# ODE stage of a mixed convolution and attention kernel: chunks 2 and 3 of the first product summed and split together

## The reference

```python
def _mlp(y, W1, b1, W2, b2, W3, b3):
    h = jnp.tanh(y @ W1.T + b1)          # 128 -> 512
    h = jnp.tanh(h @ W2.T + b2)          # 512 -> 512
    return h @ W3.T + b3                 # 512 -> 128

def _rk4_step(y, dt, params):
    k1 = f(y); k2 = f(y + dt / 2 * k1); k3 = f(y + dt / 2 * k2); k4 = f(y + dt * k3)
    return y + dt * (k1 + 2 * k2 + 2 * k3 + k4) / 6
# y0 = the layer-normed token 0 of each batch entry; 511 such steps, one after the other,
# give the 512 states that are added to the stream
```

## Time and profile before

| | |
|---|---|
| median of 3 runs | 10121.75 us (10118.84 to 10124.09) |
| the profiled execution | 10122.17 us |
| its span, first to last instruction | 10120.3 us |
| PE busy | 6818.0 us (67%) |
| DVE busy | 6894.7 us (68%) |
| ACT busy | 3280.2 us (32%) |
| POOL busy | 2146.6 us (21%) |
| mean granted TensorE clock, share of full speed | 0.623 |

### The profile page before, as it was taken

How to read it: one execution, slowest core, us unless ns; L and a number is a source line. 1 busy time by engine, 2 the same in 40 slices (tenths; PEclk the granted TensorE clock), 3 DMA queues, 4 the chain that set the end, 5 groups by cost and what they waited for, 6 DMA issues and landing times. The chain is left out here.

```text
span 10120.3 us, 368042 instructions
## 1 busy us (share of the span) xinstructions
PE 6818.0 (67%) x137720; PEld 5044.2 (50%) x137720; DVE 6894.7 (68%) x34057; ACT 3280.2 (32%) x11208; POOL 2146.6 (21%) x5931
## 2 busy tenths in 40 slices
PE   7886566666666666666666666666666558888888
PEld 3332455555555555555555555555555433333333
DVE  4554566666666666666666666666666479888898
ACT  3442222222222222222222222222222345555555
POOL 0000111111111111111111111111111025555554
PEclk8887555555555555555555555555555679999998
DMA  0000000000000000000000000000000000000000
GB/s 6 1 1 1 9 3 3 3 4 3 3 4 3 3 3 4 3 3 3 4 3 3 3 4 3 3 3 4 3 3 20 0 16 16 16 16 16 16 16 4
DMA packets 20732, 60.86 MB, mean 6 GB/s; under 512 B 4260, under 2 KB 13159, under 8 KB 16759
## 3 DMA queue, kind: packets, MB, share of 16 engines
q1 hardware_dynamic: 18502, 36.44, 1.0%
q0 software_dynamic: 432, 0.56, 0.0%
HBM read 35.94 MB, written 1.05 MB: 4 GB/s over the span
## 5 line engine op out<-in xcount | busy, mean ns | idle before, releaser
L565 PE MATMUL p<-H,W 128*128 128x8 f16 x130816 | 4162.8, 168 | 2547.1 <-DVE H L706 2536.6
L565 PEld LDWEIGHTS p<-H,W 128*128 128x128 f16 x130816 | 3816.6, 104 | 2893.3 <-DVE H L706 2882.4
L706 DVE SCALAR_TENSOR_TENSOR H<-h,H 128x8 f16<-128x8 f32 x10220 | 1499.7, 163 | 281.3
L641 ACT ACTIVATE h<-u 128x8 f32<-128x8 f32 x4088 | 852.1, 208 | 2490.3 <-DVE u L726 2297.5
L636 ACT ACTIVATE h<-r 128x8 f32<-128x8 f32 x4088 | 851.2, 208 | 2477.8 <-DVE r L734 2253.5
L726 DVE TENSOR_REDUCE u<-p 128x8 f32<-128x24 f32 x6132 | 1000.8, 174 | 826.4 <-PE p L565 826.4
L734 DVE TENSOR_REDUCE r<-p 128x8 f32<-128x24 f32 x4088 | 746.2, 183 | 1129.3 <-PE p L565 848.4
L701 DVE TENSOR_SCALAR H<-h 128x8 f16<-128x8 f32 x8176 | 1399.1, 171 | 38.4 <-ACT h L636 38.3
L1060 POOL TENSOR_TENSOR F<-F,dist 128x512 f32<-128x512 f32 x512 | 757.7, 1482 | 892.7 <-DVE F L1203 892.7
L541 POOL TENSOR_TENSOR twice<-r 128x16 f32<-128x16 f32 x511 | 109.8, 215 | 2932.5 <-DVE r L734 2932.5
L1197 DVE TENSOR_SCALAR qn<-dist 128x512 f32<-128x512 f32 x544 | 675.7, 1242 | 0.0
(11 more groups left out here) (290 smaller groups left out, 5598.1 us busy)
## 6 DMA issues: line engine op xcount, KB each, us to landing
W_even<-in_spline SPq DMA_DIRECT2D x12, 1024.0 KB, 6.9
W_odd<-in_spline SPq DMA_DIRECT2D x12, 1024.0 KB, 6.8
s<-in_scaler SPq DMA_DIRECT2D x24, 128.0 KB, 7.3
W_even<-in_base SPq DMA_DIRECT2D x12, 128.0 KB, 6.7
W_odd<-in_base SPq DMA_DIRECT2D x12, 128.0 KB, 6.6
xb<-in_x SPq DMA_DIRECT2D x4, 256.0 KB, 2.7
w2f<-in_ff_w SPq DMA_DIRECT2D x1, 1024.0 KB
out_x<-stream SPq DMA_DIRECT2D x1, 1024.0 KB, 4.2
```

Of the source, the lines that this page charges most:

```text
L565: ins = pe.matmul(out[:, m, 0:2 * B], W[:, q, k, P * m:P * m + P], H[:, k, :, :].rearrange("p q b -> p (q b)"), start=fresh[m], stop=(left ...
L641: sg.up(act.activation(cols(h2[:, e, :], q), cols(u2, q), ACT.Tanh, scale=scale), "h2")
L706: sg.up(dve.scalar_tensor_tensor(out=Hq[:, :, 1, :], in0=mb(cols(h, q)), scalar=HSCALE, in1=Hq[:, :, 0, :], op0=ALU.mult, op1=ALU.subtract ...
```

## The change

Chunks 2 and 3 are summed by one `tensor_reduce` after the first product and their low halves are written by one operation. PE raises `l2_ps` twice instead of three times in an evaluation, DVE `u2` and `in2` likewise, and ACT's second tanh waits for the second sum. The order of the blocks stays.

```diff
-    RED2, LOW2 = [(0, 1), (2,), (3,)], [(0, 1), (2,), (3,)]
+    RED2 = LOW2 = [(0, 1), (2, 3)]
...
-                                wait(act, "u2", len(RED2) * e + (1, 3)[n], w, i)
+                                wait(act, "u2", len(RED2) * e + n + 1, w, i)
...
-                        low(h2[:, e, :], H2, 2, (2,), at2 + 2, w, i)
-                        low(h2[:, e, :], H2, 2, (3,), at2 + 2, w, i)
+                        low(h2[:, e, :], H2, 2, (2, 3), at2 + 2, w, i)
```

## The result

The changed kernel takes **10148.96 us** (median of 10 runs, 10139.44 to 10159.43) against 10124.01 us for the kernel before in the same comparison (10 runs): ratio 1.0025, 95% interval 1.0016 to 1.0035. It is slower by 25 us, just clear of the noise, where 10114 us was forecast and the range ended at 10142. The profiled execution took 10142.68 us, 20.5 us more than the one before.

The account below looks back on a forecast made before the run. The ODE stage was taken as bound by a chain of small dependent steps through chunks 0 and 1. Merged sum 0, merged low half 0, code pauses -8 us from 10121.75 gave 10114 us, range 10088 to 10142.

Parts of the forecast that it names:

- The loop: PE-DVE-ACT chain through chunks 0 and 1: stays 1.62 us per product; merged sum and low half count 0 us.
- my own sign of being wrong: In the ODE stage: the first product's period differing from the second's would show the forecast wrong on the loop.
- The waits: DVE and PE signals: one wait fewer per evaluation each; ACT's second wait only gets a new number; counted 0 us.
- The code pauses: DVE's instruction supply: 80 instructions a step become 60, so pauses cost less, 8 us gained; bounds 32 gained, 16 lost.
- the queue: Rival: DVE's queue is on the loop, so removed operations gain 470 us, giving 9652 us; chance 2%.
- the longer sum: Rival: the merged sum, 13 ns longer, delays the high half behind it, 27 us slower, 10149 us; chance 5%.
- within 0.2%: Whole kernel: the time stays within 0.2% (about 20 us) of the kernel before; chance 77%.

Follow-up runs that it names:

- e1_early: The changed kernel with ACT's wait for POOL's sums (hsum) moved from the first tanh of line 641 to the second tanh of line 636; 10117.34 us.
- e5b_splits: The changed kernel with three separate sums again, only the low halves merged, and the second tanh's wait as before; 10128.38 us.
- e3_each: The changed kernel with the wait for hsum in all four evaluations of a step instead of one; 10235.03 us.
- e2_swap: The changed kernel with ACT's two waits in the other order, u2 first and hsum second; 10154.76 us.
- e4_sums: The changed kernel with only the sums merged, the low halves of chunks 2 and 3 staying two operations; 10161.35 us.
- e6b_pad2: e1_early plus two one-column memsets on DVE ahead of its loop, carried out once in the launch; 10105.45 us.
- e7b_pad4: e4_sums with the early wait of e1_early and four one-column memsets on DVE ahead of the loop; 10093.2 us.
- e8b_pad1: e4_sums with the early wait of e1_early and one one-column memset on DVE ahead of the loop; 10175.46 us.

## Why the prediction was wrong

**The loop: right, but for that one tanh.** PE starts 1.62 us apart in both products in three evaluations of four, the merged operations take 182 and 167 ns, and the freed DVE time is idle time (392 us less busy, where over 400 were forecast). In a step's first evaluation the first product takes 1.68 us (3737.89 to 3739.57 above), and a difference between the two periods was my own sign of being wrong. e1_early shows that both merged operations together cost the loop nothing; e5b_splits agrees for the low halves alone.

**The waits: the step that failed.** I wrote that "ACT's second wait has a new number and the same meaning" and counted 0. The second wait is as I said. What I passed over is ACT's first wait for `u2`: the register instruction ahead of it went away, and with it the carrier of the wait for `hsum`. I had seen that `l2_ps` would share the others' registers on DVE, priced it there as a gain, and didn't follow the same sharing into ACT's queue, where two waits stand ahead of one operation of the loop. Measured: 0.06 us x 511, 31.6 us by e1_early, 56 ns per added instruction by e3_each.

**The code pauses: right in kind, near in size.** Forecast were 60 DVE instructions a step and 8 us of gain. The stage has 26061 operations and 4585 register instructions, 60.0 a step. e1_early, which has the change without the wait, is 6 us faster than the kernel before, which the interval can't tell from nothing. The traces can. I took the starts of all 4088 products (every 32nd matmul of line 565) and summed what each takes over the usual 1.621 us, apart for the five products at each of the six ends of the unrolled loop:

| kernel | low halves of chunks 2 and 3 | six ends, us | everywhere else, us |
|---|---|---|---|
| before | separate | 31.7 | 36.7 |
| changed | merged | 38.7 | 51.9 |
| e1_early | merged | 38.7 | 24.4 |
| e2_swap | merged | 38.5 | 66.6 |
| e3_each | merged | 39.3 | 141.7 |
| e4_sums | separate | 32.2 | 66.9 |
| e5b_splits | merged | 39.7 | 39.1 |
| e6b_pad2 | merged | 39.7 | 14.3 |
| e7b_pad4 | separate | 32.4 | 0.2 |
| e8b_pad1 | separate | 32.3 | 81.9 |

"Everywhere else" is the pauses, and the wait where there is one. From the kernel before to e1_early it falls by 12 us, where 8 were forecast; from e1_early to the changed kernel it rises by 27.5, which is the wait. Sums by profile and medians of times differ by up to 9 us, since the rest of the launch does.

**A term that I hadn't.** At the six ends of the unrolled loop, where the engines jump back to its top, PE stands idle for some microseconds. The end near 2050 before, then in the changed kernel (idle time before PE's first matmul of the turn, then within its first product):

```profile
2053.41 0.72 PE L565 MATMUL p<-H,W 128*128 128x8 f16 x21 [4.33 <-DVE H L706]
...
2055.50 0.44 PE L565 MATMUL p<-H,W 128*128 128x8 f16 x11 [1.38 <-issue]
```

```profile
2056.57 0.73 PE L565 MATMUL p<-H,W 128*128 128x8 f16 x21 [4.70 <-DVE H L706]
...
2059.25 0.44 PE L565 MATMUL p<-H,W 128*128 128x8 f16 x11 [1.95 <-issue]
```

0.94 us more at this end, and 7 us over the six by the table. With it the sum closes: 27.5 for the wait, 7 for the ends, less 12 for the pauses are 22 us, where the profiles differ by 20.5 and the medians by 25. The table also says which half of the change does it: the ends take 38.5 to 39.7 us in all six kernels with the merged low half and 31.7 to 32.4 in all four without it, and e5b_splits has nothing else changed. In the six, PE has 8 register instructions a step, in the four 20. The DMA records point to the supply of code: at each of the six ends of the changed kernel one packet of 16384 bytes of instructions takes 2.0 to 2.6 us, in the kernel before 1.1 to 1.5. Why those packets get slower with less code stays open.

**The rivals.** Neither the queue (470 us faster) nor the longer sum (27 us slower) came true. The time came out near the second by another mechanism, so its 5% were no merit of the forecast; that the wait, the ends and the pauses add up to nearly its 27 us is chance. The 77% for "within 0.2%" were too sure: 31 us at 10121 is 0.3%, and one instruction in one of four evaluations is enough for it.

## What to carry to other kernels

In a loop bound by a chain of small steps, count the instructions between the last wait and the operation on the critical chain, on every engine, after each change to how often a semaphore is raised: in this program the number of raises per turn decides which waits share a register, and a shared register can take away the instruction that carried a second wait. Put a wait that is met early ahead of an operation off the loop. And before a difference of 0.3% is given to a change, move the code by a few instructions that do nothing: here that alone was worth 82 us.

## What I had not expected of the hardware

A second wait ahead of a tanh on the loop costs 56 to 60 ns, even for a semaphore that is met long before (86 us over 1533 in e3_each; the tanh 0.276 instead of 0.217 us behind its sum). The late wait then stands on an instruction of its own, whose row shows only 17 ns, less than a third of the cost. A register instruction of 35 ns in the same place cost 70 to 80 ns (e2_swap).

DVE's pauses come back every 128 instructions of its code: with 64 instructions a step in every other step (e4_sums, e8b_pad1). They cost up to 0.32 us right behind a register instruction, 0.14 us one operation further on (e4_sums), and next to nothing in e7b_pad4 (0.2 us in the table), where by my count they fall on a sum that waits for PE anyway. I put them down to the supply of code, since moving the code moves them. The DMA records bear that out. The packets of kind "instruction" on queue 14 are nearly all of 8192 bytes, and there are 110 fewer after the change. DVE and ACT have 13796 instructions fewer in the stage, which is 108 blocks of 128 (packets, MB, share; the kernel before, then the changed one):

```profile
q14 instruction: 682, 5.58, 0.2%
```

```profile
q14 instruction: 572, 4.69, 0.2%
```

In e8b_pad1 the high half right behind a register instruction comes some 0.3 us late 253 times, and each time such a packet starts 0.6 to 1.0 us after it; behind DVE's other instructions that holds for 3 in 100. A pause thus goes with the step from one block of code to the next; why it lasts as long as it does stays open.

The Trainium skill, page "Runtime: NRT & Kernel Launch", section "Instruction fetch mechanics", speaks of blocks of 256 instructions whose crossing is mostly hidden. The runs here show pauses tied to places in the code too, and differ in the number, 128, and in that they are hidden only at some places: e8b_pad1 lost 82 us to them.
